# Cross-attention of a perceiver block as one pipeline over 16 head groups instead of four batches one after the other

## What is computed

```python
def _L0_xattn_ref(x, context, context_mask, Wq, Wk, Wv, Wo, bo, g1, b1, g2, b2):
    xn = _layer_norm(x, g1, b1)
    cn = _layer_norm(context, g2, b2)
    q = (xn @ Wq.T).reshape(B, Tx, HEADS, HEAD_DIM)      # 16 heads of 32
    k = (cn @ Wk.T).reshape(B, Tc, HEADS, HEAD_DIM)
    v = (cn @ Wv.T).reshape(B, Tc, HEADS, HEAD_DIM)
    scores = jnp.einsum('bqhs,bkhs->bhqk', q, k) / np.sqrt(HEAD_DIM)
    scores = jnp.where(context_mask[:, None, None, :], scores, -jnp.inf)
    attn = jax.nn.softmax(scores, axis=-1)
    out = jnp.einsum('bhqk,bkhs->bqhs', attn, v).reshape(B, Tx, C)
    return out @ Wo.T + bo
```

## Time and profile before

| | us |
|---|---|
| median of 3 runs | 1128.05 (1119.37 to 1132.92) |
| the profiled execution, its time | 1132.17 |
| its span on the core | 1130.4 |
| up to the first row of maxima (L720 of batch 0, group 0) | 122.9 |
| from there to the sixteenth row of maxima | 621.6 |
| from there to the end of cross-attention (x updated by L606) | 29.6 |
| self-attention, experts, output | 356.3 |

### The profile page before, as it was taken

One profiled execution on the slowest core, in us unless ns is written; L12 is line 12 of the kernel. 1 busy time (PEld: TensorE's weight loads), 2 busy tenths in 40 slices (PEclk: granted clock), 3 DMA queues, 4 the chain that ended last, 5 costly groups with the idle time before them and its releaser, 6 DMA issues. The chain is left out here.

```text
span 1130.4 us, 19687 instructions
## 1 busy us (share of the span) xinstructions
PE 951.2 (84%) x8057; PEld 531.3 (47%) x8057; DVE 727.2 (64%) x1070; ACT 528.2 (47%) x790; POOL 288.1 (25%) x244
## 2 busy tenths in 40 slices
PE   5799998999998889999899999776885319999992
PEld 4554444544444444444454444343443217766760
DVE  7965466593555683655675445876666556898882
ACT  4344444434354343344444344451454507898880
POOL 2610443320233530044441044431221140000003
PEclk9899998699999699999689999868987759999997
DMA  7323222033312012412102502225700248999934
GB/s 252 97 94 80 74 57 57 1 94 77 94 46 50 20 66 84 100 42 50 38 28 70 159 9 57 57 75 181 296 1 1 78 159 336 402 393 384 391 135 130
DMA packets 48530, 136.04 MB, mean 120 GB/s; under 512 B 9708, under 2 KB 11500, under 8 KB 44600
## 3 DMA queue, kind: packets, MB, share of 16 engines
q1 hardware_dynamic: 47160, 130.58, 34.7%
q0 software_dynamic: 1280, 4.20, 1.2%
HBM read 96.96 MB, written 11.04 MB: 96 GB/s over the span
## 5 line engine op out<-in xcount | busy, mean ns | idle before, releaser
L561 DVE TENSOR_REDUCE mpart<-ps_r 128x1 f32<-128x512 f32 x192 | 126.8, 686 | 96.5 <-PE ps_r L858 95.7
L693 ACT ACTIVATE pT<-ps_s 128x1024 f32<-128x1024 f32 x128 | 128.5, 1021 | 96.3 <-PE ps_s L880 92.4
L429 POOL TENSOR_TENSOR acc_pool<-acc_pool,pT 128x1024 f32<-128x1024 f32 x60 | 142.9, 2382 | 6.2 <-ACT pT L693 1.7
L895 PE MATMUL ps_o<-pT,vals 128*32 128x128 f32 x2048 | 111.8, 313 | 22.3 <-ACT pT L693 22.2
L429 POOL TENSOR_TENSOR acc_pool<-pT 128x1024 f32<-128x1024 f32 x16 | 38.2, 2390 | 299.1 <-ACT pT L693 281.9
L554 DVE TENSOR_TENSOR k_lo<-k_f,k_hi 128x512 f16<-128x512 f32 x64 | 43.8, 688 | 103.6 <-ACT k_hi L715 103.6
L769 PE MATMUL ps_r<-wv_hi,cT_hi 128*128 128x512 f16 x256 | 98.1, 383 | 7.9 <-DVE cT_lo L469 7.6
L710 ACT ACTIVATE k_f<-ps_r,kbias 128x512 f32<-128x512 f32 x64 | 44.0, 687 | 126.2 <-PE ps_r L841 122.2
L839 PE MATMUL ps_r<-cT_hi,wk_hi 128*128 128x512 f16 x256 | 97.3, 380 | 4.7 <-DVE mpart L561 4.3
L858 PE MATMUL ps_r<-k_stack,q_stack 98*128 98x512 f16 x192 | 86.5, 450 | 16.2 <-DVE mpart L561 13.9
L770 PE MATMUL ps_r<-wv_lo,cT_hi 128*128 128x512 f16 x256 | 97.7, 382 | 0.0
(11 more groups left out here) (237 smaller groups left out, 1849.8 us busy)
## 6 DMA issues: line engine op xcount, KB each, us to landing
w_raw<-in_w SPq DMA_DIRECT2D x30, 2048.0 KB, 10.3
raw<-in_context SPq DMA_DIRECT2D x64, 256.0 KB, 2.8
k_stack<-k_hi SPq DMA_DIRECT2D x256, 64.0 KB, 2.0
k_stack<-k_lo SPq DMA_DIRECT2D x128, 64.0 KB, 2.0
slots_in<-a_zeros SPq DMA_DIRECT2D x1, 3840.0 KB, 14.8
rows_in<-slots_in SPq DMA_DIRECT2D x15, 256.0 KB, 9.8
slots_out<-m_y SPq DMA_DIRECT2D x15, 256.0 KB, 10.2
q_stack<-k_stack SPq DMA_DIRECT2D x12, 128.0 KB, 2.3
```

The costliest lines, as they stand in the source:

```text
L429: nc.gpsimd.tensor_tensor(acc_pool[:, :], pT[:, 0, :] if p == 1 else acc_pool[:, :], pT[:, p % PT, :], ALU.add).then_inc(pool_add, 1)
L561: nc.vector.tensor_reduce(mpart[:, j, kb:kb + 1], p1_bank(step, n - 1), AX.X, ALU.max).then_inc(p1_max, 1)
L693: nc.scalar.activation(pT[:, p % PT, :], ps_s[p % 2][:, :], ACT.Exp, scale=SM_SCALE).then_inc(exp_done, 1)
L895: last = nc.tensor.matmul(ps_o[g % 2][HD * j:HD * (j + 1), 0:P], vals[:, 2 * p + i, head:head + HD], pT[:, p % PT, at:at + P], start=(p == ...
```

## The change

A window is one head group of one batch: there are 16, numbered w, and group g is w % 4. The whole of cross-attention is one list of steps (`all_steps`). Window w runs the 8 pairs of its own attention, and beside each pair stands a piece of later work:

- pairs 0 and 1: keys of window w+1, blocks 2 and 3; pairs 2 to 5: values of window w+1 for its own 128 columns only, four tiles to a bank; pairs 6 and 7: keys of window w+2, blocks 0 and 1.
- pairs 2 to 6: the 16 maxima matmuls of window w+1.
- groups 0, 1 and the start of 2: statistics and normalising of the next batch, one tile a pair; group 2, pairs 3 to 7, and group 3, pair 0: its transposes, in place of the context tiles just used.

What this alters in the parts: `raw` holds 16 tiles (normalised in place), loaded 4 at a time; `vals` is two buffers of one group; `ps_s` is one buffer of two banks, so scores run one pair ahead instead of two; keys, values and `op` share two banks (`ps_a`), transposes, maxima and `mt` two others (`ps_b`). A value matmul has 128 columns where it had 512, so there are four times as many. All sums are on POOL. The first stretch (`first_steps`) makes the tiles, keys and values of window 0 and half of the keys of window 1. `halves_behind_maxima` does what `maxima_first` did, for all windows.

```diff
+def window_steps(w):
+    b, g = w // NG, w % NG
+    more, later = w + 1 < WINDOWS, w + 2 < WINDOWS
+    following = b + 1 < NB
+    p1 = [("p1", w + 1, j, kb) for h in range(2) for j in range(HPG) for kb in (2 * h, 2 * h + 1)] if more else []
...
+    for p in range(NPAIR):
+        side = [("mt", w + 1)] if p == NPAIR - 1 and more else []
+        if g == 3 and p == 0:
+            side, t = side + t, []
+        for n in range(4):
+            if g == 2 and p >= 3 and n < 3:
+                side, t = side + t[:1], t[1:]
+            if 2 <= p <= 6 and (n < 3 or p == 6):
+                side, p1 = side + p1[:1], p1[1:]
+        heavy = []
+        if more and p < 2:
+            heavy = [("k", w + 1, p + 2, c) for c in range(NC)]
+        elif more and p < 6:
+            heavy = [("v", w + 1, p - 2, i) for i in range(QUAD)]
+        elif later and p >= 6:
+            heavy = [("k", w + 2, p - 6, c) for c in range(NC)]
+        light = []
+        if following and (g < 2 or (g == 2 and p < 3)):
+            kt = NPAIR * g + p
+            light = ([("st", b + 1, kt)] if g < 2 else []) + ([("nm", b + 1, kt - 3)] if kt >= 3 else [])
...
+        nxt = [("s", w, p + 1, 0), ("s", w, p + 1, 1)] if p + 1 < NPAIR else []
+        for n in range(max(4, len(side))):
+            steps += heavy[n:n + 1] + side[n:n + 1]
+            if n == 1:
+                steps += nxt[:1] + light[:1]
+            if n == 2:
+                steps += nxt[1:] + light[1:]
+        if w and p == 1:
+            steps.append(("den", w - 1))
...
+        steps += [("av", w, p, 0), ("av", w, p, 1)]
+        if p == NPAIR - 1 and more:
+            steps += [("s", w + 1, 0, 0), ("s", w + 1, 0, 1)]
...
+def first_steps():
+    steps = []
+    for n in range(NQ):
+        tiles = range(QUAD * n, QUAD * (n + 1))
+        steps += [("st", 0, kt) for kt in tiles] + [("nm", 0, kt) for kt in tiles]
+        steps += [("t", 0, kt) for kt in tiles]
+        if n:
+            steps += [("k", 0, n - 1, c) for c in range(NC)]
...
+                    for j in range(HPG):
+                        for k, part in enumerate((k_hi[h], k_hi[h], k_lo[h])):
+                            sp.dma_start(t.k_stack[u][HD * k:HD * (k + 1), j, 2 * KB * h:2 * KB * (h + 1)],
...
+                    if j == 0 and kb % 2 == 0:
+                        pe.wait_ge(k_in[w % 2][kb // 2], (w // 2 + 1) * KIN)
...
+                    kt, col = QUAD * q + i, slice(P * g, P * (g + 1))
+                    to, keys = bank_a(step[:3])[:, P * i:P * (i + 1)], slice(P * kt, P * (kt + 1))
+                    for c in range(NC):
+                        nc.tensor.matmul(to, cT_hi[:, c, keys], t.wv_hi[:, c, col], start=(c == 0), stop=False)
```

More of the change, by code:

```diff
@@ L45 @@
 NKB = KEYS // KB
-POOL_ADDS = (5, 5, 5, 4)
-RAW = 4
 PT = 4
-def attention_steps():
-    def scores(g, p):
-        return [("s", g, p, 0), ("s", g, p, 1)]
-    steps = []
[L64 to L108, removed]
@@ L117, in maxima_first, with all_steps, halves_behind_maxima @@
+def all_steps():
+    steps = first_steps()
+    for w in range(WINDOWS):
+        steps += window_steps(w)
+    return steps + [("den", WINDOWS - 1), ("low", WINDOWS - 1)] + [("op", NB - 1, n) for n in range(NG)]
+def halves_behind_maxima(steps):
     order = list(steps)
-    for step in [step for step in steps if step[0] == "k" and step[1] > 1]:
+    for step in [step for step in steps if step[0] == "k" and step[3] == NC - 1]:
         at = order.index(step)
-        behind = [n for n in range(at + 1, min(at + 8, len(order))) if order[n][0] == "p1"][:2]
+        behind = [n for n in range(at + 1, min(at + 9, len(order))) if order[n][0] in ("p1", "t")][:2]
@@ L209, in cross_attention @@
         cT_hi, cT_lo = t.cT_hi, t.cT_lo
-        vals = sb("vals", [P, NKT, D])
+        vals = [sb(f"vals{u}", [P, NKT, P]) for u in range(2)]
         k_f = sb("k_f", [P, 2, KB])
@@ L241, in cross_attention @@
         k_in = [[sem(f"k_in{u}{h}") for h in range(2)] for u in range(2)]
-        mask_in = sem("c_mask_in")
+        mask_in = [sem(f"c_mask_in{u}") for u in range(2)]
         p1_mm, p1_max, m_max, mt_mm, m_row = (sem("p1_mm"), sem("p1_max"), sem("m_max"), sem("mt_mm"),
@@ L741, in _ @@
         @block.tensor
         def _(pe):
-            def transposes(kt, b):
-                pe.wait_ge(normed, b * NKT + kt + 1)
-                if kt >= 4:
-                    pe.wait_ge(tr_lo, b * NKT + kt - 3)
-                for c in range(NC):
-                    last = nc.tensor.transpose(t_bank(kt)[:, P * c:P * (c + 1)],
-                                               xn[:, kt % RAW, P * c:P * (c + 1)], t.ident[:, :])
-                last.then_inc(tr, 1)
-            released = {"v": v_out, "k": k_f_out, "p1": p1_max}
@@ L776, in bias_columns, with bank_b_free @@
+            def bank_b_free(step):
+                at = ring_b.index(step)
+                if at >= 2:
+                    before = ring_b[at - 2]
+                    if before[0] == "t":
+                        pe.wait_ge(tr_lo, NKT * before[1] + before[2] + 1)
+                    elif before[0] == "p1":
+                        pe.wait_ge(p1_max, nth_p1(before))
+                    else:
+                        pe.wait_ge(m_row, before[1] + 1)
+                return ps_b[at % 2]
             def bias_columns(i):
@@ L918, in one_batch @@
                         last.then_inc(op_mm, 1)
-            for b in range(NB - 1):
-                one_batch(b, in_loop)
-            one_batch(NB - 1, at_end)
 def w1_part(n):
```

818 lines of the change are left out of this document (366 added, 452 removed).

## The result

The changed kernel takes 1160.5 us, the median of 4 runs (1157.0 to 1163.7), against 1123.8 for the kernel before in the same comparison; the ratio is 1.0315 with a 95% interval of 1.0234 to 1.0397. The forecast was 1146 with a range of 1095 to 1180, slower as the likeliest case: the direction and the range hold, and the loss is about twice the one forecast. The profiled execution has a span of 1157.3 us where the forecast's sum gave 1148.4.

A forecast was written before the change was run, and what follows sets the result against it. PE, busy 574.1 of 621.6 us between first and last row of maxima, was taken as the bound; the terms summed to 1148.4 us of span, 1150 against a profiled 1132, hence 1146 in runs, range 1095 to 1180.

The forecast's parts named there:

- to the first row of maxima: Start of the kernel up to the first row of maxima: 118.6 us, against 122.9 before.
- PE's work of 15 windows: PE's work from first to sixteenth row of maxima at full clock, 35.0 us a window plus transposes and output projections: 548 us.
- waits for half 0: PE waits at each window's first maximum for key copies, 2.2 us each, about 1.8 more after group 2: 38 us.
- waits for half 1: PE waits at the ninth maximum for key copies, about 1.0 us in 11 windows: 11 us.
- clock (what is left of the stretch): Half of 15 waits bring a stretch of 5.4 us at the lower clock, losing 2.7 us each: 20 us.
- smaller waits: PE's waits in group 2, at the maxima row, for window 14's splits and DVE's normalising: 27 us, between 10 and 50.
- the end: End of cross-attention, with POOL alone adding the sums: taken as 29.5 us, against 29.6 before.
- the rest: Everything behind cross-attention, which the change does not touch: stays at 356.3 us.
- The waits for the copies: Half 0 and half 1 waits together, 38 and 11 us; for half 0, a chain of 11.8 us against 9.6 of PE work.
- DVE held up by POOL: Rival, chance 0.08: POOL's adds hold DVE's normalising of 48 tiles; a third reaching PE adds 21 us: 1167.
- no wait: Rival, chance 0.24: PE reaches the first maximum over 2.2 us later, half 0 has landed: 1087 us, faster.
- half the waits: Rival, chance 0.16: waits of 1 us at the copies, too short to lower the clock: 1102 to 1125 us.

The follow-up runs named there:

- eight: The changed kernel without the four low-half key copies of each half from window 2 on, 8 DMAs instead of 12 (computation incomplete): 1108.2 us, ratio 0.9857.
- k_early: The changed kernel with the key blocks made two pairs and more earlier, four pairs or more before the first maximum that reads them: 1115.7 us, ratio 0.9913.
- best_b: k_early plus mt_late, first-stretch key blocks ahead of transposes, window 15 sums shared by DVE and POOL, pair 6 statistics and normalising in pair 7 (groups 0, 1): 1089.0 us.
- straight: The changed kernel with DVE walking the list as it is, low halves of key blocks not put behind the next two maxima or transposes: 1197.3 us, ratio 1.0629.
- mt_late: k_early with the row of maxima made on PE after the third quarter of a window's last key block instead of the first: 1103.3 us, ratio 0.9819.
- half_sums: k_early with POOL adding only 512 of each tile's 1024 columns from window 1 on (denominators not right): 1093.6 us, ratio 0.9729.

## Why the prediction was right, term by term

The forecast's sum and what the profile of the changed kernel shows, in us:

| term | forecast | measured |
|---|---|---|
| to the first row of maxima | 118.6 | 130.8 |
| PE's work of 15 windows | 548 | 554.2 |
| waits for half 0 | 38 | 36.2 |
| waits for half 1 | 11 | 11.2 |
| clock (what is left of the stretch) | 20 | 17.0 |
| smaller waits | 27 | 19.6 |
| the end | 29.5 | 34.2 |
| the rest | 356.3 | 354.1 |
| span | 1148.4 | 1157.3 |

- **The waits for the copies**, the term that decided the case, were 47.4 against 49. The single one in the trace was 11.82 less 9.6, as the sum had it, with one issue of double length among the twelve. After a group 2 they were 3.65, 4.76 and 3.67, against 4.0 forecast. That they are the cause, and that SP's issues make them, was shown by two runs, eight and k_early.
- **PE's work.** It is read from the windows of best_b: 15 times 34.98, three times 43.92 less 34.97 for the transposes and three times 2.60 for the output projections (37.57 less 34.97), less 5.2 for the two key blocks that are missing: 554.2. The 35.0 of a plain window is right to 0.03. What I mis-sized is a transposed tile among maxima: 43.92 less 34.97 over 16 is 0.56 us and not the 0.44 of the earlier trace rows, where eight stood in a row; over 48 tiles that is the 6 us.
- **The clock.** This is a remainder: 638.2 less 67.0 of waits less 554.2 of work. I took half of 15 waits to lose it and 2.7 us each. It was six of 15, and by the stretches at a granted clock of 0.50 (3.4 us each, 5.0 behind the wait of 4.76) they cost an estimated 11 us, 1.8 each. The three other falls cost some 4 more, and the last 2 have no cause in the rows. The count was a choice between ends and not a derivation, and no row here gives a rule for it. That it is the waits that cost clock is borne out over the runs: PE's busy time in the middle, for the same work, was 591.1 us with 84.3 us of waits (straight), 571.7 with 67.0 (the changed kernel), 562.2 with 30.7 (k_early), 557.1 with 22.9 (mt_late), 556.7 with 15.1 (best_b).
- **The first stretch** is the step that failed, by 12.2 us. 6.4 of them are in the start that the sum took over from the kernel before, "tiles start to be used at 45.7": in the changed kernel PE is through with the first quad's transposes only at 52.12. Both kernels fill rows of `q_stack` with two memsets on POOL, 14 to 15 us together. Before, POOL's deviations of the first context tiles stood ahead of them; the change took these away, and so the memsets begin 12.4 us earlier and meet DVE's normalising of x. Timeline of the kernel before:

```profile
16.50 1.90 DVE L511 TENSOR_SCALAR pT<-pT,x_mv,x_rstd 128x512 f32<-128x512 f32 x4
...
29.30 15.04 POOL L410 MEMSET q_stack<- 2x8192 f16 x2
29.45 8.02 DVE L521 TENSOR_SCALAR k_stack<-mask_u 4x2048 f16<-4x2048 uint8 x1
```

  and of the changed kernel:

```profile
16.87 15.27 DVE L442 TENSOR_SCALAR pT<-pT,x_mv,x_rstd 128x512 f32<-128x512 f32 x4
16.89 14.06 POOL L370 MEMSET q_stack<- 2x8192 f16 x2
...
24.24 1.09 PE L672 MATMUL ps_s<-ident_sb,pT 128*128 128x128 f32 x4 [6.96 <-DVE pT L442]
31.30 1.12 PE L672 MATMUL ps_s<-ident_sb,pT 128*128 128x128 f32 x4 [5.97 <-DVE pT L442]
...
35.40 1.20 DVE L451 TENSOR_SCALAR k_stack<-mask_u 4x2048 f16<-4x2048 uint8 x1
```

  The four instructions took 15.27 us instead of 1.90, PE waited 12.9 us for them, and the projection of q began at 35.62 instead of 22.34. Before, the same memsets held DVE at the mask row (8.02 us, where the changed kernel has 1.20), and part of the 13 us was lost there. All runs that start from the changed kernel have this, best_b too (15.28 us). None moves the memsets, so what they cost the total is not shown by an experiment. From 52.12 to the key block at 98.62 are 46.5 us where the sum had 42.9 (three quads of 12.3, and 6), 3.6 more. There the sum put a key block at 2.6 us and left out that PE, ACT and DVE wait for each other: the block behind quad 2's transposes took 4.7 us from 83.45 on, since the granted clock was 0.61 over that quad, and its evictions and the statistics begin only behind it. The last 2.2 us arose behind 98.62.
- **The end** was 4.7 us longer than I took it for. I had seven adds of POOL in a row from 4.6 us on. They began at 4.7 us, but POOL then stood still for 4.35 us, as an exponential came late. The last five adds in the timeline, and PE at the denominators:

```profile
774.10 5.86 DVE L525 SCALAR_TENSOR_TENSOR cT_lo<-raw,cT_hi 128x512 f16<-128x512 f32 x3 [1.04 <-ACT cT_hi L624]
...
783.15 13.24 POOL L382 TENSOR_TENSOR acc_pool<-acc_pool,pT 128x1024 f32<-128x1024 f32 x5 [4.35 <-ACT pT L614]
...
797.79 0.65 PE L789 MATMUL ps_o<-acc,ones 128*32 128x128 f32 x8 [5.04 <-POOL acc L389]
```

  ACT was held at the denominators of window 14, which DVE reached behind the three splits of the first row. Alone a split takes 0.68 us; two of these three, beside POOL's adds, took 2.50 and 2.83, so some 4 of the 5.86 us are again DVE held up by POOL.
- **Smaller waits** were 7 us under the estimate. Those in group 2 were 3.2 us a batch, against 4 to 5, those in window 14 7.6.
- **DVE held up by POOL** had a chance of 0.08, for the normalising of context tiles. In the changed kernel none of that was held (0.608 us at most), and the low halves that were are off the path. But the kernel did pay for the mechanism, in places for which the sum had no term: the normalising of x at the start, three splits of window 14 ahead of its last maxima (2.48 or 2.49 us each beside an add, 0.68 alone) and the splits at the end. I had looked for it in the wrong instructions. That adds hold DVE is shown by half_sums; that the memsets do is read from the two timelines above.
- **The rivals of no wait and half the waits** fell. PE did not reach the first maximum later than the sum had it, since nothing else in pairs 0 and 1 held it up. eight, with nearly none of these waits, is near to what the first of them would have been: 1108 and not 1087, since the first stretch and the end were long in any case.

The errors do not all point one way: the first stretch, the end and the transposes were 23 us too low, the clock, the waits and the rest 14 too high. That the sum came within 9 us is partly luck. Of the 14.5 us between 1146 and 1160.5, 8.9 are the sum's; another 4.1 were taken off because the profiled execution of the kernel before lay above its median, while that of the changed kernel lay 1.4 below its own. The median of the kernel before then came out 4 us lower with the fourth run. Together these make the difference between 1.6 and 3.1%. The direction and its cause, the waits for the copies, were not luck: they were in the sum and came as large as it said.

## What to carry to other kernels

When work is put into one dense pipeline, a chain through several engines and a DMA queue no longer has slack by itself. Add up that chain from the producer's last instruction to the consumer (here evictions, twelve issues in a row and one landing: 11.8 us), add up what the critical engine does between the two (9.6), and put the producer early enough that the second is the larger; a schedule with the same work and only that distance changed was 4% faster. Then look at what stands right ahead of the next short chain (here the last maximum and its row): two held instructions there, 2.2 us longer than alone, came out as waits of 2.59 us on PE. And when steps are moved or dropped on one engine, look at what of its other work moves up (here two memsets of 7 us) and what it then runs beside.

## What the runs showed of the hardware

- DVE's `k_lo` (0.68 us) and normalising (0.54) took 1.08 us more when they began under an add of POOL (k_early), while reductions from PSUM beside the same adds stay at 0.66 to 0.69, and so do low halves of transposed tiles, which have one input in PSUM (0.68 to 0.69, all 64 in the changed kernel). With adds of half the columns, the wait behind two such instructions fell from 2.59 to 0.42 us.
- Beside a memset of POOL of 7 us it is as strong: two of the four normalising instructions of x took 7.22 us each instead of 0.54, and the mask's `tensor_scalar` 8.02 instead of 1.20. No run took the memsets away.
- A wait of 2.39 us on PE was followed by half the clock and one of 2.47 was not, and PE had the same list of work around both (windows 4 and 12). Which of the waits costs clock could not be told from their length, and I tried nothing to settle it.
- Narrow matmuls, each with its own weight load, are nearly free of extra cost: 3072 of 128 columns in place of 768 of 512 added 4 us (0 to 8) to the kernel before.
